# Attention one of a language-model tower: maxima two banks at a time, shifts behind later masks, earlier statistics

## The reference, cut to what matters

```
qkv = einsum('bhce,ef->bhcf', xh, Wqkv) + bqkv
att = einsum('bhqe,bhke->bhqk', q, k) / sqrt(16)
att = softmax(att * tril(ones, k=-1))          # masked scores are 0, not minus infinity
out = einsum('bhqk,bhke->bhqe', att, v), then out @ Wr + br
```

## Time and profile before

| what | us |
|---|---|
| time, median of 3 runs | 2953.96 (2953.74 to 2954.68) |
| profiled execution, its own time | 2954.28 |
| its span, first to last instruction | 2952.5 |
| passes 0 and 1, from the first exponential | 57.81 (from the pass's start) and 53.17 |
| passes 2 to 27 together | 1145.79 |
| an even pass and an odd pass of the loop (14, 15) | 46.53 and 42.07 |
| granted TensorE clock over the span | 0.94 |

### The profile page before, as it was taken

One profiled execution on the slowest core, in us unless ns is written; L12 is line 12 of the kernel. 1 busy time (PEld: TensorE's weight loads), 2 busy tenths in 40 slices (PEclk: granted clock), 3 DMA queues, 4 the chain that ended last, 5 costly groups with the idle time before them and its releaser, 6 DMA issues. The chain is left out here.

```text
span 2952.5 us, 58168 instructions
## 1 busy us (share of the span) xinstructions
PE 2543.3 (86%) x15254; PEld 1489.2 (50%) x15318; DVE 2114.0 (72%) x5668; ACT 1509.7 (51%) x3246; POOL 1644.1 (56%) x2564
## 2 busy tenths in 40 slices
PE   1768888888888888888876999999999979999999
PEld 0323433333443333443354666666666647666676
DVE  2656667766666776766646999999999865565554
ACT  1335555555555555555532655565555544444444
POOL 3663343433343433343244878888877757776775
PEclk7679999999999999999977999999999979999999
DMA  3343433443443443443340000000000000000000
GB/s 57 92 111 58 64 57 51 64 71 51 64 60 54 57 72 54 61 64 52 58 139 0 1 1 0 0 0 0 0 0 0 1 4 17 14 16 14 16 16 18
DMA packets 81255, 112.93 MB, mean 38 GB/s; under 512 B 25101, under 2 KB 37145, under 8 KB 80537
## 3 DMA queue, kind: packets, MB, share of 16 engines
q1 hardware_dynamic: 76360, 101.44, 20.1%
q0 software_dynamic: 3072, 8.39, 1.0%
q10 hardware_dynamic: 1744, 2.16, 0.2%
HBM read 18.98 MB, written 8.39 MB: 9 GB/s over the span
## 5 line engine op out<-in xcount | busy, mean ns | idle before, releaser
L661 DVE TENSOR_REDUCE cand<-ring 128x4 f32<-128x512 f32 x1152 | 713.5, 681 | 389.4 <-PE ring L771 369.8
L570 ACT ACTIVATE probs<-scoresT 128x512 f32<-128x512 f32 x1152 | 624.4, 605 | 624.9 <-PE scoresT L715 622.3
L491 POOL TENSOR_SCALAR_AFFINE_SELECT probs<-probs 128x256 f32<-128x256 f32 x512 | 204.8, 414 | 464.9 <-ACT probs L570 458.2
L715 PE MATMUL scoresT<-stage 98*128 98x512 bf16 (+3 forms) x1536 | 381.6, 340 | 41.8 <-ACT probs L570 28.0
L735 PE MATMUL pv<-probs,Vg 128*32 128x512 f32 (+3 forms) x3072 | 344.6, 573 | 23.8 <-POOL probs L491 18.0
L771 PE MATMUL ring<-Km,Qm 64*128 64x512 bf16 (+2 forms) x1792 | 230.3, 323 | 95.8 <-DVE cand L661 44.5
L1198 PE MATMUL mm<-w_W,hT 128*128 128x256 f32 x1024 | 243.2, 381 | 8.0 <-ACT z L1286 3.3
L1218 PE MATMUL mm<-w_W,x2T 128*128 128x512 f32 x512 | 242.7, 597 | 0.3 <-DVE x L1437 0.2
L715 PEld LDWEIGHTS scoresT<-stage 98*128 98x128 bf16 x1536 | 122.1, 99 | 219.3 <-ACT probs L570 126.6
L771 PEld LDWEIGHTS ring<-Km,Qm 64*128 64x128 bf16 x1792 | 76.5, 96 | 295.7 <-issue 120.1
L1279 ACT ACTIVATE hT<-mmT,w_be,w_g 128x128 f32<-128x128 f32 x512 | 185.5, 468 | 78.1 <-PE mmT L1209 78.1
(11 more groups left out here) (254 smaller groups left out, 5270.0 us busy)
## 6 DMA issues: line engine op xcount, KB each, us to landing
stage<-parts SPq DMA_DIRECT2D x256, 96.0 KB, 2.8
stage<-parts SPq DMA_DIRECT2D x256, 64.0 KB, 2.8
Qm<-parts SPq DMA_DIRECT2D x128, 128.0 KB, 2.6
Km<-parts SPq DMA_DIRECT2D x128, 128.0 KB, 2.7
stage<-parts SPq DMA_DIRECT2D x256, 32.0 KB, 2.4
out<-result SPq DMA_DIRECT2D x64, 128.0 KB, 1.7
stage<-ct SPq DMA_DIRECT2D x128, 4.0 KB
w_W<-in_W SPq DMA_DIRECT2D x4, 512.0 KB
```

The costliest lines, as they stand in the source:

```text
L491: nc.gpsimd.affine_select(out=d, in_=d, compare_op=ALU.is_gt, fill=0.0, base=0, pattern=[[0, 2], [1, P]], channel_multiplier=-1).then_inc( ...
L570: nc.scalar.activation(probs[:, buffer(slot), :], scoresT[slot % SCORE_BANKS][:], ACT.Exp, scale=SOFT).then_inc(exp_ok, 1)
L661: ins = nc.vector.tensor_reduce(c, src[:].rearrange("p (t a b) -> p t a b", t=c.shape[1], b=P), AX.X, ALU.max)
L715: ins = nc.tensor.matmul(scoresT[slot % SCORE_BANKS][:, at:at + hi - lo], Ks[0:ROWS, gi, hh, P * kt:P * kt + P], Qs[0:ROWS, gi, hh, lo:hi] ...
```

## The change

The 18 pairs of banks of maxima, which stood two pairs at a time at nine positions, stand one pair at a time at 0, 1, 3, 5, 6, 8, 10, 12, 13, 15, 17, 18, 20, 22, 24, 25, 27 and 29. MAX_FINAL keeps VectorE's reduction, behind the ninth pair (13) and the last (29); GpSimd's three steps become an event SHIFT of their own, at 18 for the first and, for the second, at 33, behind the mask of S33. Bursts 0 to 3 stand at 9, 12, 20 and 28, burst 4 at 1 behind a pair of maxima; PV_HALF goes from 17 to 14. XT moves from 4 and 7 to 6 and 8, the first QK from 9 to 10. In an odd pass LN_STATS moves from 20, 23, 25, 28 to 12, 15, 18, 21 and LN_POWER with its last part. The 56 gathers, which stood one to a bank over pass 0 and 20 banks of pass 1, stand two to a bank at the first 28 banks of pass 0.

```diff
--- before.py
+++ after.py
@@ -91,9 +91,7 @@
         column_ += hi_ - lo_
 
 BURSTS = [(0, (0, 1)), (0, (2, 3)), (1, (0, 1)), (1, (2, 3)), (1, (4, 5)), (1, (6, 7))]
-BURST_AT = {0: 11, 1: 15, 2: 22, 3: 30}
-
-MAX_AT = (0, 3, 7, 11, 15, 18, 22, 26, 30)
+BURST_AT = {0: 9, 1: 12, 2: 20, 3: 28}
 
 
 MASKS = ([(1, None), (2, 384), (3, 384), (5, None), (6, 384), (7, 384), (8, 256), (9, 256), (27, None), (29, None)]
@@ -140,10 +138,11 @@
 
 LN_LATER = 13
 AT = {
-    0: {"LN_NORM": (1, 2, 4, 5), "XT": (4, 7), "PV_COPY": 4, "EQ": 6, "TMP": 0, "PT": 5, "OT": 24, "WR": 25, "RSUM": 3, "SUF": 12, "QK": (9, 13, 17, 20), "MID_LAG": 2, "V": 21, "VG": 5, "LOAD": 0, "PV_HALF": 17},
-    1: {"LN_STATS": (20, 23, 25, 28), "PV_COPY": 4, "EQ": 6, "TMP": 0, "PT": 5, "WR": 2, "V": 8, "VG": 6, "LOAD": 0, "PV_HALF": 17},
+    0: {"LN_NORM": (1, 2, 4, 5), "XT": (6, 8), "PV_COPY": 4, "EQ": 6, "TMP": 0, "PT": 5, "OT": 24, "WR": 25, "RSUM": 3, "SUF": 12, "QK": (10, 13, 17, 20), "MID_LAG": 2, "V": 21, "VG": 5, "LOAD": 0, "PV_HALF": 14},
+    1: {"LN_STATS": (12, 15, 18, 21), "PV_COPY": 4, "EQ": 6, "TMP": 0, "PT": 5, "WR": 2, "V": 8, "VG": 6, "LOAD": 0, "PV_HALF": 14},
     "V_IN": 0, "WR_IN": 1,
 }
+MAX_FIRST, MAX_LAST, SHIFT_LAST = 0, 31, 33
 ALONE = {"LN_STATS": (0, 0, 0, 0), "LN_NORM": (1, 1, 1, 1), "XT": (2, 2), "QK": (8, 9, 10, 11), "MID_LAG": 1, "V": 12, "PV_COPY": 1, "TMP": 2, "PT": 5, "OT": 11,
          "WR": 14, "VG": 14, "LOAD": 14, "MX": 15}
 
@@ -167,7 +166,7 @@
             at(pos_of["LN_STATS"][n] + (0 if scores else LN_LATER * (ahead - 1)), ("LN_STATS", ahead, n))
         at(pos_of["LN_STATS"][-1] + (0 if scores else LN_LATER * (ahead - 1)), ("LN_POWER", ahead))
     if tail:
-        at(0, ("PV", -1, 4))
+        at(1 if scores else 0, ("PV", -1, 4))
         at(3 if scores else 0, ("PV", -1, 5))
         at(pos_of["PV_COPY"], ("PV_COPY", -1, 1))
         at(pos_of["TMP"], ("TMP", -1))
@@ -200,7 +199,10 @@
                     uses[-1] += [("R", "CT", "dve", p - 1)]
             uses[-1] += [("MAX_FINAL", p)] + ([("LOAD_MAX", p)] if load_max else [])
         for n, u in enumerate(uses):
-            at(MAX_AT[n // 2] if scores else pos_of["MX"] + n, *u)
+            at(MAX_FIRST + n * (MAX_LAST - MAX_FIRST) // len(uses) if scores else pos_of["MX"] + n, *u)
+            if n % MAX_BANKS == 2 and n > MAX_BANKS:
+                at(MAX_FIRST + n * (MAX_LAST - MAX_FIRST) // len(uses) if scores else pos_of["MX"] + n, ("SHIFT", 0))
+        at(SHIFT_LAST, ("SHIFT", PAIRS_MX - 1))
         at(UNITS - 1, ("R", "CT", "dve", PAIRS_MX - 1))
     if scores:
         at(pos_of["EQ"], ("EQ",))
@@ -490,8 +492,9 @@
                                     d = probs[:, buffer(slot), :].rearrange("p (a b) -> p a b", b=P)[:, 0:second // P + 1:second // P, :]
                                 nc.gpsimd.affine_select(out=d, in_=d, compare_op=ALU.is_gt, fill=0.0, base=0,
                                                         pattern=[[0, 2], [1, P]], channel_multiplier=-1).then_inc(mask_ok, 1)
-                            if section == "first" and gi * UNITS + slot < TILES - TPB:
-                                gather(TPB + gi * UNITS + slot, gat1)
+                            if section == "first" and gi == 0 and 2 * slot < TILES - TPB:
+                                gather(TPB + 2 * slot, gat1)
+                                gather(TPB + 2 * slot + 1, gat1)
                         elif kind == "LN_POWER":
                             hn = hb + e[2]
                             wait_apart(pool, (mv_ok, LN_PARTS * (hn + 1)))
@@ -520,7 +523,7 @@
                                     pool.wait_ge(rsum_c, (TPB - 2) * hb + TPB - 1 - t)
                                 else:
                                     ins.then_inc(rsum_ok, 1)
-                        elif kind == "MAX_FINAL":
+                        elif kind == "SHIFT":
                             g, par, n = G + 1, (gi + 1) % 2, PAIRS_MX * (G + 1) + e[2]
                             two = slice(2 * e[2], 2 * e[2] + 2)
                             wait_apart(pool, (m_ok, n + 1))
```

## The result

| | before | after |
|---|---|---|
| time, median of 4 runs, us | 2954.32 (2953.74 to 2954.96) | 3024.52 (3020.52 to 3025.95) |
| passes 0 and 1 | 57.8 and 53.2 | 88.3 and 38.7 |
| passes 2 to 27 | 1145.8, clock 0.94 | 1197.3, clock 0.90 |
| a pair of the loop | 88.1 | 92.1 |

The ratio is 1.0235, interval 1.0218 to 1.0253: 70 us slower, where 16 us faster was forecast. The profiled execution took 3023.96 us, with a span of 3022.2. The windows of after, from first exponential to first exponential, are those of the earlier trace rows: passes 0, 1, 14, 15 and 29, then passes 2 to 27 together. The columns are us, busy time of PE, PEld, DVE, ACT and POOL, granted clock, DMA share, GB/s.

The account below looks back on a forecast made before the run. No engine is full; the time lies in who waits for whom. Gathers +13, 13 pairs at -1.9 (39.4 + 46.8 against 88.1) -25, elsewhere -4: -16, so 2938 us; 8 in 10 from 2910 to 2964.

Parts of the forecast that it names:

- +1.2 for the falls that stay: Odd pass of the loop: remaining clock falls add 1.2 us to 38.2 at full clock, giving 39.4.
- Falls come less often at a seam where TensorE has more to do: Even pass: rarer seam falls, but 2.9 us standing is a new place for one; 46.8 us, 45.6 at full clock.
- the walk: Following the engines' lists through the loop's passes at full clock: odd pass 38.2 us, even pass 45.6.
- the gathers: Passes 0 and 1: pass 0 takes 86.4 us, 28.6 more; pass 1 37.5, 15.7 less; both +13 (0 to +20).
- The sign that the prediction itself named: Whole loop: the forecast is wrong if the granted clock leaves 0.94 by more than 0.02.
- the upper ends of both passes together: Loop: odd pass at most 40.5 us if all falls stay, even pass at most 48.3 with both falls.
- Rival 1: Even pass's new stall lowers the clock every time, bursts 0 and 1 run slow: 87.8 a pair, 2961 us; chance 0.24.
- Rivals 1 and 4: Rival 4: in the loop VectorE's idle only moves, pairs stay at 88.1, 2965 us; chance 0.07.
- The waits: TensorE stands 2.9 us before the even pass's fifth pair, 1.9 and 1.5 before the odd pass's 12th and 15th.
- The wait for ScalarE at the even pass's 12th pair: Even pass: ScalarE copies pv ahead of the third QK, the 12th pair waits for it: +0.6 us.
- VectorE's idle time in an odd pass: Odd pass of the loop: a sign, VectorE idle near 8 us, from 11.4 now.
- Elsewhere -4: Last two pairs of passes, with less of the same work: -4 us (0 to -8).

Follow-up runs that it names:

- a_fill_even: Changed kernel plus ten useless matmuls ahead of the fifth pair of maxima in each even pass: 2976.5 us, 48 less than the changed kernel.
- a_fill_all: Changed kernel plus useless matmuls ahead of even passes' fifth pair of maxima, the 12th in both, odd passes' 15th, and CT at each pass's end: 2920.73 us.
- m_stats_fill: Kernel before, maxima one pair at a time, loop's statistics at 12 to 21, gathers as before, useless matmuls ahead of four maxima pairs: 2854.0 us, ratio 0.9658.
- b_fill: Kernel before plus useless matmuls ahead of CT at each pass's end and of the 12th pair of maxima in odd passes: 2899.72 us.
- b_max_shift: Kernel before with maxima one pair at a time, plus the SHIFT event, second shift behind the mask of bank 33: 2924.9 us.
- b_max_only: Kernel before with only the maxima changed, one pair of banks at a time over positions 0 to 29: 2893.4 us.

## Why the prediction was wrong

**The step that failed** is the price of the clock's falls: "+1.2 for the falls that stay" in the odd pass, and in the even one "Falls come less often at a seam where TensorE has more to do". The forecast took 45.6 + 38.2 = 83.8 us for a pair at full clock, and 2.4 for the falls. The first figure is right: 83.1 in after, and 84.8 measured with the gaps filled. The second is not: half of 18.1, so 9.0 us a pair. 6.6 us too little in each of 13 pairs is 86 us. The rest nearly cancels: the walk was 0.7 a pair too long (-9), the gathers cost 3 more, and the last pairs and what lies around them 6 more. Together that is the miss, 3024 less 2938.

The walk through the list promised no gain by itself: at full clock the kernel before stands at 83.3 us a pair in the table, the walk at 83.8. The forecast gain of 1.9 a pair came from falls that were to cost 2.4 us where they cost 4.9 (half of 9.7). The prediction's first paragraph has 6.7 + 3.7 us at the lower clock for a pair of before; the sum that follows sets no price on that total. In after the falls cost 9.0: TensorE's waits there are shorter in all, but fewer and longer, and filling them takes the falls away.

The sign that the prediction itself named, the loop's clock leaving 0.94 by more than 0.02, is there (0.90).

The mistake has three parts. Of a fall I counted what one costs at a pass's start (1.5 us) and not how many there are. I let the seam's falls become rarer while the same text had CT wait as long as now, and a burst that no longer waits then simply ran in the fall. And I took each place by itself: a_fill_even shows the next pass's falls hanging on this one's. So even the upper ends of both passes together, 40.5 + 48.3 = 88.8, lay below the 92.1 measured, and the range with them.

**Rival 1** named the mechanism, a new wait in the even pass that lowers the clock each time, and a_fill_even shows it: filled, this place gave 45 us of loop back. It priced a pair at 87.8, because it allowed that one new place and no more. (Rivals 1 and 4 are summed with -2 for the last pairs where the forecast has -4; nothing hangs on it.)

**What held.** The gathers: 86.4 and 37.5 us forecast, 88.25 and 38.73 measured, 16 for the pair against 13; the groups of lines have the same price for each (the gathers of pass 0 in after: busy us, mean ns | idle):

```profile
L461 POOL DMA_INDIRECT h<-in_WT,tok x56 | 53.4, 954 | 14.2 <-issue 13.9
```

The waits: 2.67, 1.78 and 1.33 us where 2.9, 1.9 and 1.5 were forecast; no wait before XT; CT's wait as before at this seam, burst 4 without one. The row of burst 4's 0.74 us names ScalarE's exponential, and that it stood for masks was the prediction's reading; over the loop of before the profile puts 9.4 us of the bursts' waits down to masks and 3.7 to the exponential, and after has neither. The wait for ScalarE at the even pass's 12th pair grew by 1.0 us (1.44 against 5.9 / 13 = 0.45), where +0.6 was forecast. VectorE's idle time in an odd pass, forecast near 8 us, is 10.9 in after (41.71 less 30.78) and 8.1 with the gaps filled (38.73 less 30.68): this sign, too, hung on the clock. The four tiles' normalization beside GpSimd: 1.80 us, forecast 2.1. "Elsewhere -4" was +0.1 in the last two pairs, a small miss of the same kind.

**What the walk could not show**, since it priced the sum only: the parts are of opposite signs. At full clock, us a pair: maxima -3.0, shift +2.7, bursts +0.6, XT -0.1, statistics -0.5, together -0.3; after stands at -0.2. But the sum is no proof that they are independent: undoing the shift in after takes away CT's waits and yet gives 1.2 and not 2.7. And the low time does not add at all: the parts' differences come to about +1 us a pair, the whole change's is +8.4.

The Trainium skill's rule that the prediction set beside rival 1 ("TensorE: Matmul & The Clock Gate", section "HAM oscillation": idle gaps throttle the clock again) agrees with these runs: 455 matmuls put into the gaps held the clock at 1.00 through 1102 us. The waits that were filled are 1.1 to 2.7 us long.

**Open:** the part of half the low time that filling does not bring back (22 us in a_fill_all and m_stats_fill, 7 in a_fill_even, 2 in b_fill) may be the filling's own cost, by running over the end of the gap or by what it does to other engines, or time at the lower clock in which TensorE did not set the pace; no run parts the two. Nor is it known why b_max_shift, whose waits of TensorE in the loop come to 147 us, has only 6.6 us low a pair, why the earlier statistics spare the clock, and why the shift costs 2.7 us a pair beside the maxima alone and 1.2 in the whole change (the waits for CT differ less, 2.6 and 2.2). Of the parts, only the gathers and the shift were taken out of after.

## What to carry to other kernels

A long wait of TensorE can be paid twice, once standing and once at the lower clock behind it, and the sum of the waits doesn't tell: after waits 12 us less in the loop than before and is 51.5 us longer. Multiply each stretch's time by its granted clock to see whether an edit changed the schedule or the clock, and price falls by the time at the lower level, not by the stall that brings them. Issue the small steps that a transposition waits for before a queue's other work, not behind it: GpSimd's three steps behind the masks to bank 33 made TensorE stand in all 26 passes of the loop where it had stood in 6 (b_max_shift beside b_max_only). Where a gap can't be closed, try to fill it with useless matmuls (23 to 95 us of the loop here); and try the parts of a bundled edit one at a time, since here the maxima and the statistics without the gathers gained 79 us, and the whole cost 70.

## What the runs showed of the hardware that was not expected

Six waits of 1.1 to 2.7 us in a pair of 92 us (two at seams, two in the even pass, two in the odd), 9.4 us in all, were enough to hold TensorE at the lower level for 18 us of it, a fifth of the time; filled, it was never there. Filling a gap in one pass removed time at the lower level in the next as well (a_fill_even: odd passes 1.5 us shorter, nothing changed in them). And the low times of edits are not additive: beside the maxima alone, four edits that change them by between -1.5 and +3.5 us a pair, some +2.5 by their sum, give +10.0 together.
